# Node-row products of a graph kernel: the table in two float32r parts, and the cycles that use them

## The chip, the cores and the metric

The kernel runs on 1 core of one Trainium2 chip. The metric is the device time of one execution in microseconds (us), as the median of several runs.

## The reference, cut to what matters

There are 3125 nodes with 128 features and 53125 edges, sorted by their target node. The layer that is computed is

```python
row, col = (edge_index[0], edge_index[1])
h = jnp.concatenate([x[row], edge_attr], axis=1)
h = jax.nn.relu(_bn(h @ W1 + b1, g1, be1))
s = jax.ops.segment_sum(h, col, num_segments=n)
...
agg = jnp.where(cnt > 0, s / jnp.maximum(cnt, 1.0), 0.0)
h2 = jnp.concatenate([x, agg], axis=1)
h2 = jax.nn.relu(_bn(h2 @ W2 + b2, g2, be2))
return jax.nn.relu(h2 @ Wl + bl)
```

and the result is the layer norm of x plus that. `_bn` is a batch norm over all rows, so the mean and variance over all edges must be known before the segment sums start.

## The kernel before, in words

Since `x[row] @ W1x` is the same as picking rows of `x @ W1x`, the kernel first forms the table y = x W1x (3125 rows of 128), keeps it in SBUF as `ysb` and writes it to DRAM as `ytab`. The edges are then handled in 26 cycles (`NI`) of 4 groups (`U`), a group being 4 tiles of 128 edges: 416 tiles in all. For a tile, the rows of y come in one of three ways:

- the 12 tiles of the first three groups are gathered from x itself (line 642), before the table is ready;
- most others are gathered from `ytab` by an indirect DMA that GpSimd issues (`gather`, line 660), one instruction for each tile, all in one fixed order over cycles and groups;
- in the cycles of `NODES`, one or two tiles of group 2 (`NODEQ`) are not gathered. `node_onehots` (VectorE, line 1243) compares the node number of each edge with each of the 25 slices of nodes, which gives a one-hot matrix of 125 rows for each slice, in five batches; `node_rows` (TensorE, line 757) multiplies the 25 slices of `ysb` with them and sums in PSUM; `rows_out` (ScalarE, line 1039) copies the sum; `rows_back` (line 765) turns it and adds it to the edge product. Before, a pair of tiles is handled so in cycles 2 to 15 and a single one in cycles 16 to 19: 32 tiles.

In each group TensorE multiplies the edge attributes (`product`, line 744), VectorE adds the gathered rows (`make_h`, lines 1219, 1227, 1228 and 1230) and sums h and its squares (1251, 1258), and ScalarE makes the squares (984). `gather(i, q)` waits until the h of the same group of the cycle before is made (`h_ready`), so GpSimd can be up to four groups ahead of VectorE. In cycles 1 to 14 one more product for each cycle, x W2x for a part of the nodes (`x_product`, line 817), is made and copied by `x_product_out` (998). `onehots` (1209) makes the one-hots of the targets; from cycle 2 on it reads its constants from PSUM, where `keep_in_psum` (1289, 1290) puts them in cycle 1.

After the last cycle come the statistics, then the segment sums (line 890, from 497 us on), then the node part and the output. This second half is not touched.

The order of work on each engine is written out by hand, with semaphores between them. SBUF is full: the table, the one-hots and the node numbers lie in the tail of `res`, in slots that later cycles fill with h.

Of the kernel before, what the change touches and what calls it, by code (L numbers as in the profile page):

```python
# [26 lines left out]
F32 = mybir.dt.float32  # L27
BF16 = mybir.dt.bfloat16
I32 = mybir.dt.int32
ALU = mybir.AluOpType  # L30
ACT = mybir.ActivationFunctionType
AX_X = mybir.AxisListType.X

P = 128
# [5 lines left out]
KEEP = 3  # L40
# [3 lines left out]
EARLY = 3  # L44
QUAD = 32
ROWS0 = 2
ROWS1 = 20
PAIRS1 = 16
NODEQ = 2


# [5 lines left out]
def gnn_kernel(nc, E, x, xt, src, src_rows, dst, dst_rows, ea, W1, b1, g1, be1, W2, b2, g2, be2, Wl, bl, out):  # L57
    N, F = x.shape
    NI, FE = ea.shape[0], ea.shape[1] // 2
    H2 = W2.shape[1] // P  # L60
    NT = 25
    PN = N // NT
# [13 lines left out]
    BATCH = [(t, min(4, NT - t)) for t in range(0, NT, 4)]  # L76
# [10 lines left out]
    with ctx:  # L87
        def sb(name, shape, dt=F32):
            return ctx.enter_context(nc.sbuf_tensor(name, shape, dt))
# [4 lines left out]
        def sem(name):  # L94
            return ctx.enter_context(nc.semaphore(name))

        GF = TILES * F
        res = sb("res", [P, NI * KEEP * GF])
        work = sb("work", [P, 6, GF])
        away = [work[:, 0, :], work[:, 1, :]]  # L100
# [43 lines left out]

        at = NI * KEEP * GF

        def tail(n):
            nonlocal at
            at -= n
            return res[:, at:at + n]  # L150

        ysb = tail(NT * F)
        NODES = range(ROWS0, ROWS1)
        NODEAT = [P * sum(node_tiles(m) for m in range(i)) for i in range(ROWS1 + 1)]
        srcz = tail(NODEAT[-1] // 2).bitcast(BF16)
        TAB0 = at
        xt0 = tail(N)
        XT0 = at
# [43 lines left out]
        XW = XP * NT  # L202
        XSTEPS = [(h, k, min(XP, PN - k)) for k in range(0, PN, XP) for h in range(H2)]
# [1 line left out]
        h2x = agg[:, 3 * GF:3 * GF + XW]  # L205
        xgt = [agg[:, (1 + k) * GF:(2 + k) * GF] for k in range(2)]
        sq = [agg[:, (4 + k) * GF:(5 + k) * GF] for k in range(2)]
        assert XW <= 512 and len(XSTEPS) <= XT0 // (KEEP * GF) - 1

        psT = [pb(f"psT{i}", [P, 512]) for i in range(2)]  # L210
        psH = [pb(f"psH{i}", [P, GF]) for i in range(2)]
# [4 lines left out]
        psP = [psH[0], psH[1], psT[0], psC[1]]  # L216
# [3 lines left out]
        nodep = psC[0][0:PN, (U + 1) * WIN:(U + 1) * WIN + NT]  # L220
        NODECUT = [(t, t + 5) for t in range(0, NT, 5)]
        NB5 = len(NODECUT)
        NODEROWS = 12
        srcn = res[:, NODEROWS * KEEP * GF:NODEROWS * KEEP * GF + NODEAT[-1]]
        LONE = TAB0 - NT * P
        lone_hot = res[:, LONE:TAB0]
        pair_hot = res[:, LONE - 2 * NT * P:LONE]
        assert LONE - 2 * NT * P >= PAIRS1 * KEEP * GF and LONE >= ROWS1 * KEEP * GF
        assert NODEROWS * KEEP * GF + NODEAT[-1] <= PAIRS1 * KEEP * GF

        def node_chunk(i, b):

            t0, t1 = NODECUT[b]
            w = node_tiles(i) * P
            return (pair_hot if i < PAIRS1 else lone_hot)[0:PN, t0 * w:t1 * w]

# [39 lines left out]
        s_ysb = sem("y_ready")  # L276
        s_zr = sem("zeros_ready")
        s_tab = sem("table_written")
        x_ps = sem("w2_x_psum")
        x_out = sem("w2_x_copied")  # L280
        x_saved = sem("w2_x_saved")
# [14 lines left out]
        cnt_placed = sem("cnt_rows_placed")  # L296
# [413 lines left out]
        def _(pe):  # L710
# [10 lines left out]
            for b, (t0, n) in enumerate(BATCH):  # L721
# [7 lines left out]
                for t in range(n):  # L729
                    last = pe.matmul(psH[b % 2][0:PN, t * F:(t + 1) * F], xtv[:, t0 + t, :], w1x[:, :],  # L730
                                     start=True, stop=True)
# [5 lines left out]
            def product(i, par, nth, q):  # L737
                g = U * i + q
                if q == 0:
                    pe.wait_ge(ea_loaded[par], 16 * nth)  # L740
                pe.wait_ge(h_ready, g - U + 1)
                more = q == NODEQ and i in NODES
                for b in range(2):
                    last = pe.matmul(psP[q][:, b * 2 * F:(b + 1) * 2 * F], ea_cols(par, q, b),  # L744
                                     w1e[:, :, :].rearrange("p a f -> p (a f)"), start=(b == 0 or not more),
                                     stop=not more)
                last.then_inc(prod_ready, 1)

            def node_rows(i):

                w = node_tiles(i) * P
                pe.wait_ge(h_ready, U * (i - 1) + 2)
                for b, (t0, t1) in enumerate(NODECUT):
                    pe.wait_ge(nhot_ready, NB5 * (i - ROWS0) + b + 1)
                    for t in range(t0, t1):
                        k = (t - t0) * w
                        last = pe.matmul(psP[1][:, 0:w], ysb[0:PN, t * F:(t + 1) * F], node_chunk(i, b)[:, k:k + w],  # L757
                                         start=(t == 0), stop=(t == NT - 1))
                    last.then_inc(nhot_used, 1)

            def rows_back(i):
# [40 lines left out]
            def counts(i, par):  # L802

                pe.wait_ge(hotb_ready, i + 1)
                if i:
                    pe.wait_ge(cnt_placed, i)
                    pe.wait_ge(x_out, min(i, len(XSTEPS)))
                for j in range(TILES):
                    last = pe.matmul(psT[1][:, 0:U * WIN].rearrange("p (q w) -> p q w", q=U), onesb[:, :],  # L809
                                     hot[par][:, :, j * WIN:(j + 1) * WIN], start=(j == 0), stop=(j == TILES - 1))  # L810
                last.then_inc(cnt_ps, 1)

            def x_product(m):

                h, k, n = XSTEPS[m]
                pe.wait_ge(cnt_placed, m + 1)
                pe.matmul(psT[1][:, 0:n * NT].rearrange("o (p t) -> o p t", t=NT), w2x[:, h * P:(h + 1) * P],  # L817
                          xtv[:, :, k:k + n].rearrange("f t p -> f p t"), start=True, stop=True).then_inc(x_ps, 1)

            def edge_step(i, par, nth):  # L820
                if i in NODES:
                    node_rows(i)
                else:
                    product(i, par, nth, 1)
                if i <= len(XSTEPS):
                    x_product(i - 1)
                product(i, par, nth, 2)
                product(i, par, nth, 3)
                if i + 1 < NI:
                    product(i + 1, 1 - par, (i + 1) // 2 + 1, 0)  # L830
                counts(i, par)
                if i in NODES:
                    pe.wait_ge(rows_kept, i - ROWS0 + 1)
                    product(i, par, nth, 1)
                    rows_back(i)
# [32 lines left out]
            for j in range(TILES):  # L868
                h = away[1][:, j * F:(j + 1) * F]
                pe.matmul(gram, h, h, start=False, stop=False)  # L870
                last = pe.matmul(psT[0][:, 0:1], h, ones[:, :], start=False, stop=(j == TILES - 1))
# [29 lines left out]
            with pe.Else():  # L901
# [3 lines left out]
                          stop=True).then_inc(g_base, 1)  # L905
                with pe.Fori(0, NG) as g:
                    with pe.Fori(0, NB) as b:
                        pe.wait_ge(g_m, g + 1)
                        pe.wait_ge(g_hot, NB * g + b + 1)
                        for j in range(TILES):  # L910
                            pe.matmul(psH[0][:, 0:WIDE], mx[:, 0, j * F:(j + 1) * F], ghot[:, j * WIDE:(j + 1) * WIDE],
                                      start=(j == 0), stop=(j == TILES - 1))
                        for j in range(TILES):
                            last = pe.matmul(psH[1][:, 0:WIDE], onesf,
                                             ghot[:, j * WIDE:(j + 1) * WIDE], start=(j == 0), stop=(j == TILES - 1))
# [5 lines left out]
            for h in range(H2):  # L921
                last = pe.matmul(psX[:, 2 * F + h:2 * F + h + 1], w2[:, h * P:(h + 1) * P], c(C_U), start=True,
                                 stop=True)
# [39 lines left out]
        def _(act):  # L963
# [5 lines left out]
            for b, (t, n) in enumerate(BATCH):  # L969
                act.wait_ge(s_yps, b + 1)  # L970
                act.activation(ysb[0:PN, t * F:(t + n) * F], psH[b % 2][0:PN, 0:n * F], ACT.Copy).then_inc(s_ysb, 1)

            def x_rows_out(q):

# [5 lines left out]
            def squares(i, q):  # L980

                g = U * i + q
                act.wait_ge(h_ready, g + 1)
                act.activation(sq[g % 2], slot(i, i % 2, q), ACT.Square).then_inc(sq_ready, 1)  # L984

            def hot_out(i, par):

                act.wait_ge(hotb_ready, i + 1)
                act.dma_start(hot_dram[bass.ds(i, 1), :, :].rearrange("a p w -> (a p) w"),
                              hot[par][:, :, :].rearrange("p q w -> p (q w)")).then_inc(hot_saved[par], 16)  # L990

            def x_product_out(m):

                h, k, n = XSTEPS[m]
                act.wait_ge(x_ps, m + 1)
                if m:
                    act.wait_ge(x_saved, 16 * m)
                act.activation(h2x[:, 0:n * NT], psT[1][:, 0:n * NT], ACT.Copy).then_inc(x_out, 1)
                act.wait_ge(x_out, m + 1)
                act.dma_start(h2x_dram[:, h, k * NT:(k + n) * NT], h2x[:, 0:n * NT]).then_inc(x_saved, 16)  # L1000
# [40 lines left out]
            for i in range(1, NI - 1):  # L1041
                if i in NODES:
                    rows_out(i)
                if i <= len(XSTEPS):
                    x_product_out(i - 1)
                squares(i, 0)
                hot_out(i, i % 2)
                place_counts(i)
                for q in range(1, U):
                    squares(i, q)  # L1050
# [101 lines left out]
        def _(dve):  # L1152
# [132 lines left out]
            def keep_in_psum():  # L1285

                dve.wait_ge(xg_copied, EARLY)
                dve.wait_ge(s_node, 1)
                dve.tensor_copy(iotap, iota[:, :])
                dve.tensor_scalar(nodep, nodeid[0:PN, :], nodeid[0:PN, 0:1], -1.0, ALU.subtract, ALU.mult  # L1290
                                  ).then_inc(consts_kept, 1)
                dve.wait_ge(consts_kept, 1)
                dve.wait_ge(s_srcz, 1)

# [240 lines left out]
```

## Time and profile before

| | |
|---|---|
| Median of 3 runs | 634.95 us (634.64 to 634.95) |
| Profiled execution, first to last instruction (span) | 631.8 us |
| TensorE matmul busy | 503.7 us, 80% |
| VectorE busy | 464.6 us, 74% |
| GpSimd busy | 403.6 us, 64% |
| ScalarE busy | 201.2 us, 32% |
| Granted TensorE clock, mean | 0.873 of full speed |

The time of the profiled execution outside its span is not given; the median of the runs is 3.1 us above the span. Busy time leaves out what an engine spends on issuing and waiting. TensorE runs at the full clock from 55 to about 310 us, in a mix of both levels to about 376 us, at half clock to about 485 us, and at full again in the second half.

### The profile page before, as it was taken

What the parts mean: (1) busy time and instruction counts of PE and PEld (TensorE: products, weight loads), DVE (VectorE), ACT (ScalarE), POOL (GpSimd) and SP (SyncE); (2) the same over time, 40 slices, a digit from 0 to 9 for tenths busy, and PEclk for the clock granted to TensorE, in tenths of its full rate; (3) what the DMA queues carried; (4) which work ended last, traced back from release to release, by engine and by line L of the source; (5) the groups of instructions that cost most, each with busy time, mean ns of one, the idle gap of its engine ahead of it and who ended that gap; (6) DMA issues with size and microseconds to landing.
All of it is one profiled execution on the core that took longest, in us unless ns stands there. A gap on an engine that the chain in (4) does not pass through costs nothing.

```text
span 631.8 us, 9631 instructions
## 1 busy us (share of the span) xinstructions
PE 503.7 (80%) x2681; PEld 412.7 (65%) x2681; DVE 464.6 (74%) x720; ACT 201.2 (32%) x537; POOL 403.6 (64%) x507
## 2 busy tenths in 40 slices
PE   4749999999999999997866634444456899999984
PEld 4637778777777778886664422222223799999674
DVE  4789988888888998987666454454444777777786
ACT  2242222222222222222211211121114566666475
POOL 4777777777777777777777777777777133333500
PEclk9879999999999999999777755555557999999997
DMA  7953344434443434444334342334224277777103
GB/s 202 324 167 121 115 135 135 137 117 138 137 122 116 126 111 138 126 121 121 102 119 121 87 150 78 96 118 121 85 70 120 74 235 228 223 237 231 33 2 101
DMA packets 47608, 84.35 MB, mean 133 GB/s; under 512 B 11721, under 2 KB 23288, under 8 KB 47447
## 3 DMA queue, kind: packets, MB, share of 16 engines
q1 hardware_dynamic: 28834, 47.98, 23.6%
q0 software_dynamic: 12288, 25.19, 15.9%
q10 hardware_dynamic: 6453, 10.79, 4.8%
q8 instruction: 15, 0.25, 0.2%
q14 instruction: 18, 0.15, 0.1%
HBM read 63.82 MB, written 20.08 MB: 133 GB/s over the span
## 4 chain that ended last, share of the span: by engine, by line
PE 53%; POOL 24%; issue 9%; DVE 8%; DMA 3%; ACT 1%; SPq 1%; POOLq 0%; ACTq 0%; DVEq 0%
PE psH L757 25%; POOL res L660 17%; PE psH L890 7%; PE psC L890 7%; POOL work L660 7%; PE psH L744 4%; PE psT L817 3%; PE psT L744 2%; PE psC L744 2%; DVE res L1230 2%; DMA work<-ytab,srci 2%; DVE res L1387 1%; PE psT L809 1%; DMA w1x<-in_L_gnn_W 1%; DVE res L1243 1%
## 5 line engine op out<-in xcount | busy, mean ns | idle before, releaser
L660 POOL DMA_INDIRECT res<-ytab,srci x268 | 253.9, 947 | 81.7 <-issue 79.5
L757 PE MATMUL psH<-res 125*128 125x256 f32 (+1 forms) x900 | 178.7, 359 | 7.0 <-DVE res L1230 7.0
L757 PEld LDWEIGHTS psH<-res 125*128 125x128 f32 x900 | 154.9, 191 | 28.0 <-DVE res L1230 10.7
L660 POOL DMA_INDIRECT work<-ytab,srci x104 | 98.2, 944 | 31.7 <-issue 31.4
L1243 DVE TENSOR_TENSOR res<-res,psC 125x1280 f32<-125x1280 bf16 (+1 forms) x90 | 116.8, 1333 | 0.8 <-ACT res L1030 0.8
L744 PE MATMUL psH<-w1e,work 128*128 128x256 f32 x200 | 69.0, 480 | 42.8 <-DVE res L1230 42.8
L984 ACT ACTIVATE agg<-res 128x512 f32<-128x512 f32 x78 | 49.1, 630 | 143.7 <-DVE res L1230 80.5
L1230 DVE TENSOR_TENSOR res<-psH,res 128x512 f32<-128x512 f32 x50 | 34.5, 689 | 76.5 <-DMA res<-ytab,srci 48.6
L1355 DVE TENSOR_TENSOR work<-res,psX 128x512 f32<-128x512 f32 x103 | 70.2, 687 | 19.5 <-PE psC L890 12.2
L744 PEld LDWEIGHTS psH<-w1e,work 128*128 128x128 f32 x200 | 44.4, 239 | 56.5 <-issue 42.5
L685 POOL TENSOR_TENSOR agg<-agg,srci 128x64 f32 x104 | 32.0, 308 | 70.9 <-ACT srci L1095 70.0
L1258 DVE TENSOR_TENSOR psX<-agg,psX 128x512 f32<-128x512 f32 x103 | 71.0, 689 | 0.0
L1251 DVE TENSOR_TENSOR psS<-res,psS 128x512 f32<-128x512 f32 x78 | 54.3, 696 | 2.7
L890 PE MATMUL psH<-work 128*128 128x128 f32 (+1 forms) x416 | 50.8, 275 | 1.5 <-DVE work L1355 1.5
L890 PE MATMUL psC<-work 128*128 128x128 f32 (+1 forms) x416 | 50.7, 275 | 0.0
L890 PEld LDWEIGHTS psH<-work 128*128 128x128 f32 x416 | 48.5, 192 | 1.9 <-DVE work L1355 1.2
L744 PE MATMUL psC<-w1e,work 128*128 128x256 f32 x100 | 32.7, 458 | 21.0 <-DVE work L1230 21.0
L890 PEld LDWEIGHTS psC<-work 128*128 128x128 f32 x416 | 48.5, 192 | 0.0
L744 PEld LDWEIGHTS psT<-w1e,work 128*128 128x128 f32 x100 | 22.2, 232 | 40.1 <-DVE res L1230 25.0
L744 PE MATMUL psT<-w1e,work 128*128 128x256 f32 x100 | 33.1, 462 | 16.4 <-DVE res L1230 13.4
L744 PEld LDWEIGHTS psC<-w1e,work 128*128 128x128 f32 x100 | 21.5, 226 | 30.0 <-DVE work L1230 27.0
L984 ACT ACTIVATE agg<-work 128x512 f32<-128x512 f32 x25 | 15.7, 630 | 77.5 <-DVE work L1230 77.5
(200 smaller groups left out, 518.7 us busy)
## 6 DMA issues: line engine op xcount, KB each, us to landing
work<-in_edge_attr SPq DMA_DIRECT2D x26, 512.0 KB, 3.7
spill<-work SPq DMA_DIRECT2D x26, 256.0 KB, 2.3
res<-spill SPq DMA_DIRECT2D x25, 256.0 KB, 3.1
res<-ytab,srci POOLq DMA_INDIRECT x268, 2.5
hot_dram<-hotb ACTq DMA_DIRECT2D x13, 256.0 KB, 2.7
hot_dram<-work ACTq DMA_DIRECT2D x13, 256.0 KB, 2.4
hotb<-hot_dram SPq DMA_DIRECT2D x13, 256.0 KB, 2.7
work<-hot_dram SPq DMA_DIRECT2D x13, 256.0 KB, 3.0
```

The lines of the kernel that those rows point to most:

```text
L660: pool.indirect_dma_start(rows[:, j * F:(j + 1) * F], None, ytab, bass.IndirectOffsetOnAxis(ap=srci[:, j, g:g + 1], axis=0)).then_inc(gath ...
L685: pool.tensor_tensor(w, w, wsum[:, q, :], ALU.add).then_inc(agg_added, 1)
L744: last = pe.matmul(psP[q][:, b * 2 * F:(b + 1) * 2 * F], ea_cols(par, q, b), w1e[:, :, :].rearrange("p a f -> p (a f)"), start=(b == 0 or ...
L757: last = pe.matmul(psP[1][:, 0:w], ysb[0:PN, t * F:(t + 1) * F], node_chunk(i, b)[:, k:k + w], start=(t == 0), stop=(t == NT - 1))
L817: pe.matmul(psT[1][:, 0:n * NT].rearrange("o (p t) -> o p t", t=NT), w2x[:, h * P:(h + 1) * P], xtv[:, :, k:k + n].rearrange("f t p -> f p ...
L890: last = pe.matmul(psA[q][:, 0:n], mx[:, q, j * F:(j + 1) * F], hotf[:, q, j * WIN:j * WIN + n], start=(j == 0), stop=(j == TILES - 1))
L984: act.activation(sq[g % 2], slot(i, i % 2, q), ACT.Square).then_inc(sq_ready, 1)
L1230: dve.tensor_tensor(h, psP[q][:, :], h, ALU.add).then_inc(h_ready, 1)
L1243: dve.tensor_tensor(node_chunk(i, b).rearrange("p (t e) -> p t e", t=t1 - t0), srcz[0:PN, NODEAT[i]:NODEAT[i] + w].unsqueeze(1).broadcast_ ...
L1251: last = dve.tensor_tensor(psS[:, :], slot(i, par, q), psS[:, :], ALU.add)
L1258: last = dve.tensor_tensor(psX[:, :], sq[g % 2], psX[:, :], ALU.add)
L1355: dve.tensor_tensor(tiles(mx[:, q, :]), tiles(hin), negu, ALU.max).then_inc(m_ready, 1)
```

## The change

- The table is kept as two parts of type float32r in a new tile `table`: part 0 is a copy of `ysb` rounded to that type (ScalarE, right after `ysb` is complete), part 1 is the difference of `ysb` and part 0 (VectorE, in `keep_in_psum`). The one-hots are float32r too. `node_rows` issues two matmuls for each slice of nodes, one for each part, where it issued one in float32.
- The second part takes 3200 more columns of SBUF. With them the cycles move: pairs in cycles 2 to 13 (`PAIRS1` 14), singles in cycles 14 to 17 (`ROWS1` 18): 28 tiles.
- `x_product` runs twice in each of the cycles 1 to 7, where it ran once in each of the cycles 1 to 14. The second one comes after `product(i, 3)`; ScalarE copies it after the square of group 0.
- `ysb` and the node numbers (`srcn`) move to other places of `res`.

```diff
-ROWS1 = 20
-PAIRS1 = 16
+ROWS1 = 18
+PAIRS1 = 14
...
-        ysb = tail(NT * F)
+        tail(2 * NT * F)
+        table = nc.alloc_sbuf_tensor_at("node_table", [P, 2, NT * F], F32R, offset=res_at + 4 * at)
...
-        lone_hot = res[:, LONE:TAB0]
-        pair_hot = res[:, LONE - 2 * NT * P:LONE]
+        lone_hot = nc.alloc_sbuf_tensor_at("lone_hot", [P, NT * P], F32R, offset=res_at + 4 * LONE)
+        pair_hot = nc.alloc_sbuf_tensor_at("pair_hot", [P, 2 * NT * P], F32R, offset=res_at + 4 * (LONE - 2 * NT * P))
+        YAT = 20
+        ysb = res[:, YAT * GF:YAT * GF + NT * F]
...
-                        last = pe.matmul(psP[1][:, 0:w], ysb[0:PN, t * F:(t + 1) * F], node_chunk(i, b)[:, k:k + w],
-                                         start=(t == 0), stop=(t == NT - 1))
+                        for part in range(2):
+                            last = pe.matmul(psP[1][:, 0:w], table[0:PN, part, t * F:(t + 1) * F],
+                                             node_chunk(i, b)[:, k:k + w], start=(t == 0 and part == 0),
+                                             stop=(t == NT - 1 and part == 1))
...
-                    pe.wait_ge(x_out, min(i, len(XSTEPS)))
+                    pe.wait_ge(x_out, min(2 * i, len(XSTEPS)))
...
-                if i <= len(XSTEPS):
-                    x_product(i - 1)
+                if 2 * i <= len(XSTEPS):
+                    x_product(2 * i - 2)
                 product(i, par, nth, 2)
                 product(i, par, nth, 3)
+                if 2 * i <= len(XSTEPS):
+                    x_product(2 * i - 1)
...
+            act.wait_ge(s_ysb, len(BATCH))
+            act.activation(table[0:PN, 0, :], ysb[0:PN, :], ACT.Copy).then_inc(s_high, 1)
...
-                if i <= len(XSTEPS):
-                    x_product_out(i - 1)
+                if 2 * i <= len(XSTEPS):
+                    x_product_out(2 * i - 2)
                 squares(i, 0)
+                if 2 * i <= len(XSTEPS):
+                    x_product_out(2 * i - 1)
...
                 dve.tensor_scalar(nodep, nodeid[0:PN, :], nodeid[0:PN, 0:1], -1.0, ALU.subtract, ALU.mult
                                   ).then_inc(consts_kept, 1)
+                dve.wait_ge(s_high, 1)
+                dve.tensor_tensor(table[0:PN, 1, :], ysb[0:PN, :], table[0:PN, 0, :], ALU.subtract)
```

## Rows read from the trace of the kernel before

**Rows 1.** The page: chain that ended last, shares of the span.
```profile
PE 53%; POOL 24%; issue 9%; DVE 8%; DMA 3%; ACT 1%; SPq 1%; POOLq 0%; ACTq 0%; DVEq 0%
```

**Rows 2.** The chain in order of time, three of its pieces: start us, us, what.
```profile
170.29 11.06 PE psH L757 x50
187.91 11.06 PE psH L757 x50
...
256.96 11.06 PE psH L757 x50
273.18 11.06 PE psH L757 x50
```

**Rows 3.** Windows, gathers of line 660 alone: stretch, its length, busy (count), clock.
```profile
31.90:187.95 156.05, 117.97 (x125) 0.98 0.43 131
187.98:289.09 101.11, 76.44 (x81) 1.00 0.42 124
289.10:487.60 198.50, 150.05 (x159) 0.64 0.36 107
```

**Rows 4.** Groups by line, GpSimd: count, busy, mean ns, idle before and releasers.
```profile
L660 POOL DMA_INDIRECT res<-ytab,srci x268 | 253.9, 947 | 81.7 <-issue 79.5 <-DVE work L1230 0.9 <-DVE res L1230 0.9
L660 POOL DMA_INDIRECT work<-ytab,srci x104 | 98.2, 944 | 31.7 <-issue 31.4 <-DVE res L1230 0.3
```

**Rows 5.** Timeline, 20 to 47 us, GpSimd and VectorE: start us, us, engine, line.
```profile
20.55 0.94 POOL L642 DMA_INDIRECT res<-in_x,srci  x1 [0.30 <-DVE col L1196]
21.11 1.23 DVE L1209 TENSOR_TENSOR hotb<-iota,loc 128x1024 bf16<-128x1024 f32 x1
21.80 1.35 POOL L642 DMA_INDIRECT res<-in_x,srci  x1 [0.30 <-issue]
23.45 0.95 POOL L660 DMA_INDIRECT work<-ytab,srci  x1 [0.30 <-issue]
...
29.58 1.22 DVE L1209 TENSOR_TENSOR work<-iota,loc 128x1024 bf16<-128x1024 f32 x1
29.70 1.91 POOL L660 DMA_INDIRECT res<-ytab,srci  x1 [0.30 <-issue]
31.91 0.94 POOL L660 DMA_INDIRECT res<-ytab,srci  x1 [0.30 <-issue]
...
38.15 0.94 POOL L660 DMA_INDIRECT res<-ytab,srci  x1 [0.30 <-issue]
38.17 0.24 DVE L1290 TENSOR_SCALAR psC<-nodeid 125x25 f32<-125x25 f32 x1
39.25 7.08 DVE L1243 TENSOR_TENSOR res<-res,psC 125x1280 f32<-125x1280 bf16 x5 [0.84 <-ACT res L1030]
39.40 0.94 POOL L660 DMA_INDIRECT res<-ytab,srci  x1 [0.30 <-issue]
...
46.25 0.68 DVE L1230 TENSOR_TENSOR res<-psH,res 128x512 f32<-128x512 f32 x1
```

**Rows 6.** Timeline, the last gather and the add that waits for it.
```profile
487.62 0.94 POOL L660 DMA_INDIRECT work<-ytab,srci  x1 [0.30 <-issue]
...
490.32 0.69 DVE L1230 TENSOR_TENSOR work<-psC,work 128x512 f32<-128x512 f32 x1 [1.19 <-DMA work<-ytab,srci]
```

**Rows 7.** ScalarE: its timeline around 20 us, and a group by line.
```profile
16.83 0.81 ACT L971 ACTIVATE res<-psH 125x512 f32<-125x512 f32 x2 [0.28 <-PE psH L730]
21.44 0.60 ACT L978 ACTIVATE agg<-psC 128x512 f32<-128x512 f32 x1 [3.81 <-PE psC L781]
...
L1070 ACT ACTIVATE agg<-cnt,ones 128x1664 f32<-128x1664 f32 x2 | 3.3, 1674 | 0.0
```

**Rows 8.** Groups by line and form: count, busy, mean ns, idle before.
```profile
L1243 DVE TENSOR_TENSOR res<-res,psC 125x1280 f32<-125x1280 bf16 x70 | 101.2, 1481 | 0.8 <-ACT res L1030 0.8
L1243 DVE TENSOR_TENSOR res<-res,psC 125x640 f32<-125x640 bf16 x20 | 15.6, 815 | 0.0
```

**Rows 9.** Windows, all engines: PE, PEld, DVE, ACT, POOL busy (count), clock, DMA.
```profile
170.30:187.90 17.60, 17.27 (x76) 13.79 (x76) 15.81 (x20) 4.34 (x11) 13.21 (x14) 1.00 0.41 127
364.00:384.00 20.00, 9.12 (x20) 5.29 (x20) 10.33 (x16) 3.38 (x8) 15.10 (x17) 0.53 0.38 122
```

**Rows 10.** Timeline of one pair cycle and its neighbour.
```profile
169.55 0.69 DVE L1230 TENSOR_TENSOR res<-psH,res 128x512 f32<-128x512 f32 x1 [1.66 <-PE psH L744]
...
176.76 0.94 POOL L660 DMA_INDIRECT res<-ytab,srci  x1 [0.30 <-DVE work L1230]
...
203.28 0.60 PE L809 MATMUL psT<-hotb,onesb 128*128 128x256 bf16 x4
```

**Rows 11.** Timeline, the first gather of group 1 in cycle 2.
```profile
54.38 0.94 POOL L660 DMA_INDIRECT res<-ytab,srci  x1 [0.30 <-issue]
```

More of the change, by code:

```diff
@@ L29 @@
 I32 = mybir.dt.int32
+F32R = mybir.dt.float32r
 ALU = mybir.AluOpType
@@ L97, in gnn_kernel @@
         GF = TILES * F
+        res_at = -(-nc.sbuf_base // 32) * 32
         res = sb("res", [P, NI * KEEP * GF])
@@ L207, in gnn_kernel @@
         sq = [agg[:, (4 + k) * GF:(5 + k) * GF] for k in range(2)]
-        assert XW <= 512 and len(XSTEPS) <= XT0 // (KEEP * GF) - 1
+        assert XW <= 512 and len(XSTEPS) % 2 == 0 and len(XSTEPS) // 2 <= XT0 // (KEEP * GF) - 1
         psT = [pb(f"psT{i}", [P, 512]) for i in range(2)]
@@ L222, in gnn_kernel @@
         NB5 = len(NODECUT)
-        NODEROWS = 12
+        NODEROWS = 11
         srcn = res[:, NODEROWS * KEEP * GF:NODEROWS * KEEP * GF + NODEAT[-1]]
         LONE = TAB0 - NT * P
-        lone_hot = res[:, LONE:TAB0]
-        pair_hot = res[:, LONE - 2 * NT * P:LONE]
+        lone_hot = nc.alloc_sbuf_tensor_at("lone_hot", [P, NT * P], F32R, offset=res_at + 4 * LONE)
+        pair_hot = nc.alloc_sbuf_tensor_at("pair_hot", [P, 2 * NT * P], F32R, offset=res_at + 4 * (LONE - 2 * NT * P))
+        YAT = 20
+        ysb = res[:, YAT * GF:YAT * GF + NT * F]
+        assert YAT * GF + NT * F <= NODEROWS * KEEP * GF
         assert LONE - 2 * NT * P >= PAIRS1 * KEEP * GF and LONE >= ROWS1 * KEEP * GF
@@ L278, in gnn_kernel @@
         s_tab = sem("table_written")
+        s_high = sem("table_high_ready")
         x_ps = sem("w2_x_psum")
@@ L815, in x_product @@
                 h, k, n = XSTEPS[m]
-                pe.wait_ge(cnt_placed, m + 1)
+                pe.wait_ge(cnt_placed, m // 2 + 1)
+                if m % 2:
+                    pe.wait_ge(x_out, m)
                 pe.matmul(psT[1][:, 0:n * NT].rearrange("o (p t) -> o p t", t=NT), w2x[:, h * P:(h + 1) * P],
```

## The prediction, made before the changed kernel was run

> **What bounds the kernel now.** I began with the chain that ended last. It gives TensorE over half the span [rows 1], and in time order it is one node product of 11.06 us after another, 17.6 us apart and later 16.2 us apart [rows 2]. Read alone, this says that cheaper node products shorten the kernel. So I looked next at whoever else is never free. GpSimd is "busy" only 64%, but the windows that count its gathers alone say more [rows 3]: 125 gathers in 156.05 us, 81 in 101.11 us, 159 in 198.50 us, which is 1.248 us for each in all three stretches, while TensorE's clock goes from full to 0.64. The groups by line show why it looks idle: 372 gathers of 0.946 us, and before nearly every one 0.30 us put down to "issue"; the few releases put down to VectorE make 2.1 us in 372 and are the same 0.30 each [rows 4]. From 23.45 us to the last gather at 487.62 us [rows 5, 6] the queue never waits for another engine. Its pace is 464.17 us for 371 steps; less the one long step (29.70 to 31.91, 2.21 us [rows 5]) it is 461.96/370 = 1.2485 us.
>
> The chain shows TensorE because a pair cycle has 14 gathers, 14 x 1.2485 = 17.48 us, and TensorE takes 17.61 [rows 2]: it lags by 0.13 us more each cycle, and the chain prefers the later one. But that lag never reaches the queue. The gather at 176.76 may start once the h of the same group of the cycle before is made, and that was made by 169.55 + 0.69 = 170.24 [rows 10]: 6.5 us of cover. After the x products end, TensorE needs 16.2 us and catches up. So up to 488 us the time is a count: gathers times 1.2485 us, plus whatever makes one gather longer.
>
> **The change, part by part.**
>
> *Four more gathers.* 28 tiles come from node products where 32 did; the other 4 are gathered: 376 instead of 372. 4 x 1.2485 = **+5.0 us** on the queue, with nothing to cover it: behind the last gather comes the add at 490.32 that waits for its landing [rows 6], and the statistics.
>
> *The split on VectorE.* The new subtraction (125 x 3200, both inputs in SBUF) has two effects. Its length: the one-hot instruction takes 1.481 us at 1280 columns and 0.815 at 640 [rows 8], 1.04 ns a column, so 1.48 + 1920 x 0.00104 = 3.48 us. It runs right behind L1290 (38.17 to 38.41 [rows 5]), from about 38.3 or 38.4 to 41.8 or 41.9. So the one-hots start 2.6 us later than 39.25, and h of group 1 of cycle 1 is ready at about 46.25 + 0.68 + 2.6 = 49.5 [rows 5]; the gather that waits for it starts at 54.38 [rows 11]. Hidden, with 4.8 us to spare, and VectorE then has 15.8 us of work in 17.6 [rows 9] and catches up.
>
> The other effect is on the gathers themselves. Three kinds of length stand in rows 5: 0.94, 1.35 and 1.91. The two long ones are those that start while L1209 reads `iota` and `loc`, both in SBUF: VectorE ends at 21.11 + 1.23 = 22.34 and 29.58 + 1.22 = 30.80, the gathers end at 23.15 and 31.61, both 0.81 us behind it. The gather at 20.55 was under way when L1209 began and kept 0.94. So a gather wants something that this instruction holds, about 0.94 - 0.81 = 0.13 us after its start, and waits for its end. The later L1209s read the constants from PSUM, and no gather in rows 3 is longer. For the subtraction: the gather at 38.15 wants it at 38.28, the next one starts at 39.40. If the first is through, the next ends at 41.8 + 0.81 = 42.6 where it ended at 40.34: **+2.3 us**. If the subtraction is first, the one at 38.15 is caught: it ends at 42.6 instead of 39.09, +3.5 us. The two starts are some 0.1 us apart; I take the first, since L1290 is still running at 38.28, and keep both.
>
> The Trainium skill (SBUF — State Buffer, section Who interferes with whom) says that a VectorE instruction with two SBUF inputs blocks a GpSimd instruction that reads SBUF, but also that a tensor_tensor was not seen to stall the descriptor generation of a DMA. The rows speak for the first (by it 7.3 us in all); by the second the sum would be 5.0.
>
> *The copy on ScalarE.* 3200 elements; 1664 take 1.67 us [rows 7], so about 3.1 us. ScalarE is free from 17.64 to 21.44, 3.8 us of idle [rows 7]: hidden with 0.7 us left. If it were longer by a microsecond, the first h would come later, still ahead of its gather.
>
> *float32r products.* Not in the trace. A float32 product of 256 columns counts as two entries of 0.221 us (11.06/50 [rows 2]); now each part is one product, again 50 a cycle. Lower bound: the bfloat16 product of 256 columns, four in 0.60 us [rows 10], 0.15 each, 50 x 0.15 = 7.5 us. Upper bound: each still costs what float32 costs, 0.442 us, 22.1 us. I take the lower, 3.6 us less for TensorE than now, as the nearest row for one pass. It brings nothing, as the queue is ahead. It decides only when TensorE's cycle passes 17.48 us: it is 17.61 now, and 1.4 more with a second x product (17.61 - 16.21 [rows 2]), so in cycles 2 to 7 at 17.48 = 19.0 - 11.06 + 50 t, t = 0.191 us. If nothing changed at all (t = 0.221), cycles 2 to 7 would lag 1.5 us each, 9 us in all, against the 6.5 us of cover: some 2.7 us more.
>
> *One-hots in float32r.* Same columns, still 4 bytes: 0. VectorE has 17.48 - 15.81 = 1.67 us spare in a pair cycle [rows 9], so the five instructions could each be 0.33 us longer (1.81 for 1.48) before this shows.
>
> *x products in seven cycles.* Their second wait on ScalarE's copy sits ahead of product(i+1, 0), counts and product(i, 1) on TensorE; behind those waits only the h of group 1, which has the 6.5 us cover. ScalarE is 4.3 us busy in 17.6 [rows 9]. 0. The tail behind the last gather stays.
>
> *The clock.* With fewer columns TensorE may be granted the half clock at times, as later (0.53, 9.1 us busy in 20 [rows 9]). The queue kept 1.248 us there. At half clock all of a pair cycle would take about 2 x (19.0 - 11.06 + 7.5) = 31 us, more than 17.48, so TensorE would then be busy without a pause, and in the rows such stretches have the full clock: a passing lag, within the cover.
>
> **Sum.** 5.0 + 2.3 = 7.3 us. Span 631.8 + 7.3 = 639.1; the median stands 3.1 us above the span, so 634.95 + 7.3 = **642.2 us**, slower by 1.1%.
>
> **Rivals.** A measurement of this kernel can tell about 0.2%, 1.3 us, from no change.
>
> 1. *Forecast*: the queue counts, and the subtraction holds one gather. 642.2, or 643.4 if it catches the one at 38.15. Chance 0.72.
> 2. *The subtraction holds nothing*: only the four gathers, 634.95 + 5.0 = 639.9. For it: only two gathers in rows 5 show the hold. Against: both end the same 0.81 us behind VectorE. Chance 0.12.
> 3. *TensorE or VectorE takes over*: float32r products over 0.191 us, or slower one-hots. At t = 0.221, 642.2 + 2.7 = 645; at 0.442, a pair cycle takes 17.61 - 11.06 + 22.1 = 28.65, 12 x 11.2 = 134 us more, and 6 x 1.4 = 8 for the x products: about 784. Chance 0.09, mostly near the low end.
> 4. *Faster*: the shorter node products relieve the gathers. For it: the chain names TensorE in the pair cycles. Against: a gather costs 1.248 beside a full TensorE and a half empty one [rows 3]. It decides from 1.2485 x 372/376 = 1.235 us a gather if the hold is nil; with it, 8.6 us (7.3 and 1.3) must come from 376 gathers, 0.023 us each, a step of 1.226 us; then 633.6. Chance 0.04.
> 5. *No change*: something covers the four gathers, such as ScalarE's last copies ending later than the last add. The add at 490.32 is waited for directly [rows 6]. Chance 0.03.
>
> Slower 0.93, same 0.03, faster 0.04. The range takes in rivals 1 and 2 and the low end of 3: 639.4 to 645.0.
>
> **What would show it right or wrong.** In the profile after: 376 gathers at 1.2485 us; one of about 3.2 us near 39.4 (or 4.4 at 38.15); node products far shorter than 11.06 us; the last gather near 494.9; the chain in the pair cycles naming GpSimd. If the gather near 39.4 takes 0.94, rival 2 holds; if releases by VectorE of more than 0.3 us appear in GpSimd's idle time, rival 3. The forecast is wrong if the pace of the gathers depends on something that the change touches and that these windows do not vary.

## The result, and the profile after

The changed kernel takes 642.07 us (641.81 to 642.31, 4 runs), against 634.80 us for the kernel before in the same comparison: a ratio of 1.0126, 95% interval 1.0109 to 1.0143. It is slower by 7.3 us; 642.2 us was predicted.

The page of the changed kernel, its first line, the shares of the chain that ended last, and some groups (count, busy and mean; idle before and releasers):

```profile
span 640.5 us, 9412 instructions
...
POOL 51%; PE 20%; issue 17%; DVE 6%; DMA 4%; ACT 1%; POOLq 0%; ACTq 0%; DVEq 0%
...
L765 PE MATMUL psH<-pair_hot,node_table 125*128 125x256 f32 x600 | 82.1, 301 | 18.0 <-DVE res L1247 18.0
...
L1260 DVE TENSOR_TENSOR pair_hot<-res,psC 125x1280 fp32r<-125x1280 bf16 x60 | 86.6, 1479 | 0.0
```

The chain has gone from TensorE 53% [rows 1] to GpSimd 51%, while TensorE's busy time fell from 503.7 to 452.4 us. TensorE has nearly gone from the first half of the chain, and yet the kernel ends later. The one-hots cost what they cost (1479 ns for 1481 [rows 8]). The groups of GpSimd's gathers:

```profile
L667 POOL DMA_INDIRECT res<-ytab,srci x272 | 260.7, 959 | 82.9 <-issue 82.3 <-DVE res L1245 0.6
L667 POOL DMA_INDIRECT work<-ytab,srci x104 | 98.2, 944 | 31.7 <-issue 30.8 <-DVE res L1247 0.9
```

376 gathers for 372 [rows 4], the waits the same 0.30 us each, and a mean of 959 ns for 947 in one group: some gather is much longer. The timeline near 38 us shows it:

```profile
38.04 0.23 DVE L1307 TENSOR_SCALAR psC<-nodeid 125x25 f32<-125x25 f32 x1
38.19 3.48 DVE L1310 TENSOR_TENSOR node_table<-res,node_table 125x3200 fp32r<-125x3200 f32 x1
38.29 4.20 POOL L667 DMA_INDIRECT res<-ytab,srci  x1 [0.30 <-issue]
...
42.79 0.94 POOL L667 DMA_INDIRECT res<-ytab,srci  x1 [0.30 <-issue]
```

The subtraction takes 3.48 us. The gather that starts 0.10 us behind it takes 4.20 us instead of 0.94 and ends at 42.49, 0.82 us behind the subtraction, as both long gathers of rows 5 ended 0.81 us behind theirs. The end of the first half, to be read against rows 6:

```profile
496.13 0.94 POOL L667 DMA_INDIRECT work<-ytab,srci  x1 [0.30 <-issue]
...
499.03 0.69 DVE L1247 TENSOR_TENSOR work<-psC,work 128x512 f32<-128x512 f32 x1 [1.44 <-DMA work<-ytab,srci]
```

The last gather starts 8.51 us later than before (487.62 [rows 6]; 494.9 was forecast for it): 4 x 1.2485 = 4.99 for the count, 4.20 - 0.94 = 3.26 for the held gather, and 0.26 for small shifts in the first 32 us and in the steps. The span is 8.7 us longer, the median only 7.3. In every execution of this study for which both are known, 1.7 to 2.1 us lie outside the span, so the profiled execution of before, with its 631.8 us, took some 633.6 us and was about 1.3 us faster than its median.

### The profile page after: what moved, and what is told of

The parts are those of the page before. It is cut to its first block, busy times and chain, and to the rows that moved or that the text cites. A ratio compares the mean times of both kernels' runs of the same rounds, so it can differ in the third digit from the quotient of the medians.

```text
span 640.5 us, 9412 instructions
## 1 busy us (share of the span) xinstructions
PE 452.4 (71%) x2573; PEld 366.1 (57%) x2573; DVE 455.5 (71%) x709; ACT 202.6 (32%) x536; POOL 411.1 (64%) x511
## 4 chain that ended last, share of the span: by engine, by line
POOL 51%; PE 20%; issue 17%; DVE 6%; DMA 4%; ACT 1%; POOLq 0%; ACTq 0%; DVEq 0%
POOL res L667 36%; POOL work L667 13%; PE psH L903 7%; PE psC L903 7%; DMA res<-ytab,srci 2%; POOL res L649 2%; PE psH L751 1%; PE psH L765 1%; DVE res L1406 1%; DMA srci<-in_src 1%; DMA work<-ytab,srci 1%; DVE res L1247 1%; PE psT L828 1%; PE psT L968 1%; PE psH L968 1%
## 5 line engine op out<-in xcount | busy, mean ns | idle before, releaser
L667 POOL DMA_INDIRECT res<-ytab,srci x272 | 260.7, 959 | 82.9 <-issue 82.3
L751 PE MATMUL psH<-w1e,work 128*128 128x256 f32 x200 | 77.2, 526 | 74.3 <-DVE res L1247 74.3
L751 PEld LDWEIGHTS psH<-w1e,work 128*128 128x128 f32 x200 | 47.7, 262 | 103.7 <-issue 86.1
L765 PE MATMUL psH<-pair_hot,node_table 125*128 125x256 f32 x600 | 82.1, 301 | 18.0 <-DVE res L1247 18.0
L765 PEld LDWEIGHTS psH<-pair_hot,node_table 125*128 125x128 f32 x600 | 79.6, 209 | 20.5 <-DVE res L1247 20.5
L1260 DVE TENSOR_TENSOR pair_hot<-res,psC 125x1280 fp32r<-125x1280 bf16 x60 | 86.6, 1479 | 0.0
L751 PE MATMUL psC<-w1e,work 128*128 128x256 f32 x100 | 37.3, 510 | 28.6 <-DVE work L1247 28.6
L751 PE MATMUL psT<-w1e,work 128*128 128x256 f32 x100 | 35.3, 487 | 24.8 <-DVE res L1247 21.5
L751 PEld LDWEIGHTS psC<-w1e,work 128*128 128x128 f32 x100 | 23.2, 249 | 40.6 <-DVE work L1247 37.3
L1027 ACT ACTIVATE cnt<-psT 1x64 f32 x104 | 22.4, 216 | 62.9 <-PE psT L818 39.9
```

What stands on the lines that cost most here:

```text
L667: pool.indirect_dma_start(rows[:, j * F:(j + 1) * F], None, ytab, bass.IndirectOffsetOnAxis(ap=srci[:, j, g:g + 1], axis=0)).then_inc(gath ...
L765: last = pe.matmul(psP[1][:, 0:w], table[0:PN, part, t * F:(t + 1) * F], node_chunk(i, b)[:, k:k + w], start=(t == 0 and part == 0), stop= ...
L1027: last = act.activation(cnt[r:r + 1, bass.ds(bases[q], WIN)], psT[1][r:r + 1, q * WIN:(q + 1) * WIN], ACT.Copy)
L1260: dve.tensor_tensor(node_chunk(i, b).rearrange("p (t e) -> p t e", t=t1 - t0), srcz[0:PN, NODEAT[i]:NODEAT[i] + w].unsqueeze(1).broadcast_ ...
```

## The experiments

The seven kernels were timed in two batches, each on one chip together with the kernel before. Its median was 634.29 us in the batch of four (float32 with 28 tiles, two x products, pieces, subtraction twice) and 634.37 in the batch of three. Each cost over before is the difference of medians within a batch. The changed kernel was not timed again with them: where one of them is compared with its 642.07 us, the medians of the kernel before differ by 0.4 to 0.5 us, and the figure against each one's own kernel before is given too.

**The moved cycles without float32r.** The kernel before with 28 tiles and two x products a cycle, on TensorE and in ScalarE's copies. (The x products must be doubled for it: the one-hots of the first single cycle lie where `xt0` lay and wait for the last x product, which would come too late.)

```diff
-ROWS1 = 20
-PAIRS1 = 16
+ROWS1 = 18
+PAIRS1 = 14
...
-                if i <= len(XSTEPS):
-                    x_product(i - 1)
+                if 2 * i <= len(XSTEPS):
+                    x_product(2 * i - 2)
                 product(i, par, nth, 2)
                 product(i, par, nth, 3)
+                if 2 * i <= len(XSTEPS):
+                    x_product(2 * i - 1)
...
```

> The kernel before with the cycles of the change (28 tiles, two x products a cycle) but with the float32 table and float32 one-hots: no split, node products of 11.06 us. If the count of gathers sets the time, 4 x 1.2485 = 5.0 us over before, about 639.8 us, and 376 gathers in the profile with none over 2 us. If the node products on TensorE set the time, this kernel must be slower than the changed one (642.1), by up to 12 x 4.8 = 58 us, since its node products take 11.06 us where the changed kernel's take 6.26. The rival in which TensorE's lag eats the cover (19.0 us a cycle in cycles 2 to 7) gives up to 2.7 us more, 642.5.

Measured: 642.96 us (641.80 to 647.83), ratio 1.0146 (1.0118 to 1.0174), 8.7 us over before; just above 642.5, the upper end of what was expected. So TensorE's 4.8 us a cycle are not worth 58 us, and 5.0 of the 8.7 are the gathers, if each costs its step. Beside them the trace has two real waits, 3.9 us beyond the usual 0.30 each. This is the longer one, in GpSimd's timeline:

```profile
142.63 0.94 POOL L660 DMA_INDIRECT res<-ytab,srci  x1 [0.30 <-issue]
145.92 0.95 POOL L660 DMA_INDIRECT res<-ytab,srci  x1 [2.35 <-DVE res L1236]
```

A gather that waits 2.35 us, 2.05 more than the others, for an h that TensorE's lag made late. The changed kernel has no such row. In this trace the steps of the gathers also took 1.251 us instead of 1.2485, 0.9 us in all, for a reason that no run shows.

**Two x products a cycle, alone.** The same x-product edits on the kernel before, with its 32 tiles.

> The kernel before with two x products in each of cycles 1 to 7 and nothing else changed (32 tiles, float32). TensorE's pair cycle grows from 17.6 to about 19.0 us in cycles 2 to 7, with a lag of 1.5 us a cycle, 9 us in all against 6.5 us of cover. If the cover is as read, 0 to 2.7 us over before, 634.8 to 637.5. If the second wait on ScalarE's copy reaches the gathers each cycle, more than that. Gathers: 372 at 1.2485 us.

Measured: 639.28 us, ratio 1.0082 (1.0070 to 1.0094), 5.0 us over before; outside what was expected. Its chain between 107 and 147 us (start us, us, what), and one of the three gathers that wait:

```profile
107.93 11.06 PE psH L757 x50
118.99 1.88 PE psT L819 x2
...
122.59 1.88 PE psT L819 x2
...
127.49 11.06 PE psH L757 x50
```

```profile
127.70 0.94 POOL L660 DMA_INDIRECT res<-ytab,srci  x1 [2.39 <-DVE res L1236]
```

A pair cycle takes 127.49 - 107.93 = 19.56 us, not 19.0: the second x product costs 1.95 us (19.56 - 17.61), about its 1.88. In the rows left out stand only products on TensorE, one add on VectorE (0.70 us) and 0.06 us of issue: the second wait for ScalarE's copy, the other cause named in the expectation, is not in the chain. I had read 1.4 from 17.61 - 16.21 [rows 2], but the cycles that are 16.2 us apart still hold a small x product, of 125 columns where the others have 500. TensorE's timeline of the kernel before, between the node products of rows 2:

```profile
251.65 0.64 PE L817 MATMUL psT<-res,agg 128*128 128x125 f32 x2
...
267.86 0.64 PE L817 MATMUL psT<-res,agg 128*128 128x125 f32 x2
```

With 19.56 the lag is 19.56 - 17.48 = 2.08 us a cycle. The waits put down to VectorE in this kernel sum to 6.6 us over three gathers, 5.7 beyond the usual 0.30 each. What the cover was is read at the first gather of group 1 in cycle 3 and the h of the cycle before that it needs. First the kernel before, then this one, then the one with 28 tiles:

```profile
63.86 0.69 DVE L1230 TENSOR_TENSOR res<-psH,res 128x512 f32<-128x512 f32 x1 [1.73 <-PE psH L744]
71.85 0.94 POOL L660 DMA_INDIRECT res<-ytab,srci  x1 [0.30 <-issue]
```

```profile
68.07 0.69 DVE L1236 TENSOR_TENSOR res<-psH,res 128x512 f32<-128x512 f32 x1 [3.19 <-PE psH L744]
71.68 0.94 POOL L660 DMA_INDIRECT res<-ytab,srci  x1 [0.30 <-issue]
```

```profile
66.74 0.69 DVE L1236 TENSOR_TENSOR res<-psH,res 128x512 f32<-128x512 f32 x1 [3.19 <-PE psH L744]
71.99 0.94 POOL L660 DMA_INDIRECT res<-ytab,srci  x1 [0.30 <-issue]
```

The cover is 7.30 us before, 2.92 here and 4.56 with 28 tiles: the second x products of cycles 1 and 2 have taken most of the difference before the waits begin. From that h to the one of cycle 6 there are four cycles of lag, 8.3 us (both x products of cycle 7 are small). A gather that waits starts some 0.3 us after its h, so 2.92 - 0.27 = 2.65 us of cover can be used up, and 8.3 - 2.65 = 5.7 is what was measured. The 1.6 us more of cover with 28 tiles go with waits that are 1.8 us shorter; what makes it more there was not looked into.

**The subtraction in seven pieces.**

```diff
-                dve.tensor_tensor(table[0:PN, 1, :], ysb[0:PN, :], table[0:PN, 0, :], ALU.subtract)
+                for a in range(0, NT * F, 512):
+                    z = min(a + 512, NT * F)
+                    dve.tensor_tensor(table[0:PN, 1, a:z], ysb[0:PN, a:z], table[0:PN, 0, a:z], ALU.subtract)
```

> The changed kernel with the subtraction cut into seven instructions of at most 512 columns, the same work in all. If a VectorE instruction with two inputs in SBUF holds a gather until the instruction ends, a piece of 0.69 us can hold one gather by at most 0.7 us each, and the gather of 4.20 us near 38.3 shrinks to 0.94 to 1.7: about 1.5 to 3 us under the changed kernel, 639.3 to 640.6. If the gather is held by the whole backlog of VectorE, pieces or not, nothing changes: 642.1. If the long gather has another cause, 642.1 as well.

Measured: 640.01 us, ratio 1.0087 (1.0074 to 1.0100), 5.7 us over before and 2.1 us under the changed kernel (1.6 under, each against its own kernel before). VectorE and the gathers beside it:

```profile
39.46 3.98 DVE L1312 TENSOR_TENSOR node_table<-res,node_table 125x512 fp32r<-125x512 f32 x7
39.96 0.99 POOL L667 DMA_INDIRECT res<-ytab,srci  x1 [0.30 <-issue]
41.26 0.95 POOL L667 DMA_INDIRECT res<-ytab,srci  x1 [0.30 <-issue]
```

VectorE works longer (3.98 us for 3.48) with no pause between the pieces, and the gathers keep 0.95 to 0.99 us. The one at 39.96 ends at 40.95, 0.81 us behind the first piece, which ends at 40.14 while the others still have to run: a waiting gather gets in between two instructions. The one at 41.26 starts together with a piece and is not held at all; that piece takes 0.72 us instead of 0.68. Against the float32 kernel with the same 28 tiles and x products, timed in the same batch, it is 2.95 us faster: that is what the lighter float32r products are worth here, with the hold nearly gone.

**The subtraction twice.** The second writes its result, which nobody reads, beside `ysb`.

```diff
                 dve.tensor_tensor(table[0:PN, 1, :], ysb[0:PN, :], table[0:PN, 0, :], ALU.subtract)
+                dve.tensor_tensor(res[0:PN, 20 * GF + NT * F:20 * GF + 2 * NT * F], ysb[0:PN, :], table[0:PN, 0, :], ALU.subtract)
```

> The changed kernel with a second subtraction of the same size behind the first, its result not used. If the hold lasts for one instruction and the gather gets in between, the next gather is held by the second one: about 2.2 us more, 644.3. If the waiting gather does not get in between, it is held for both: 3.4 more, 645.5. If the hold is no cost of the subtraction, no change, since VectorE's extra 3.4 us lies within the cover: 642.1.

Measured: 644.03 us (642.71 to 645.62), ratio 1.0155 (1.0139 to 1.0170), 2.0 us over the changed kernel (2.5 over, each against its own kernel before).

```profile
38.25 3.48 DVE L1310 TENSOR_TENSOR node_table<-res,node_table 125x3200 fp32r<-125x3200 f32 x1
38.41 4.13 POOL L667 DMA_INDIRECT res<-ytab,srci  x1 [0.30 <-issue]
41.65 3.49 DVE L1311 TENSOR_TENSOR res<-res,node_table 125x3200 f32<-125x3200 f32 x1
42.85 3.11 POOL L667 DMA_INDIRECT res<-ytab,srci  x1 [0.30 <-issue]
```

Two gathers are held, each by one instruction: the first gets through at the seam at 41.7 and the second, started at 42.85, is held by 3.11 - 0.94 = 2.17 us until 0.82 us behind the second subtraction (45.14).

**A long instruction added to the kernel before, with two SBUF inputs, and with one.** Its result is not used.

```diff
                 dve.wait_ge(consts_kept, 1)
+                dve.tensor_tensor(res[0:PN, 20 * GF:20 * GF + NT * F].rearrange("p (t f) -> p t f", f=WIN),
+                                  ysb[0:PN, :].rearrange("p (t f) -> p t f", f=WIN),
+                                  iota[0:PN, :].unsqueeze(1).broadcast_to([PN, 2 * NT, WIN]), ALU.subtract)
                 dve.wait_ge(s_srcz, 1)
```

The other kernel has `iotap`, the same constants in PSUM, in the place of `iota`.

> The kernel before with one added VectorE subtraction of 125 x 3200 elements in keep_in_psum, with both inputs in SBUF (the constants iota as second input), its result not used. If such an instruction holds a gather until it ends, one gather near 38 to 40 us takes 3.2 to 4.3 us and the kernel is 2.3 to 3.4 us over before, 637.1 to 638.2. If only VectorE's lost time counted, it is hidden in the cover: 634.8.

> As the run with two SBUF inputs, but the second input is the copy of the same constants in PSUM. Same columns, so about the same 3.5 us on VectorE. If two SBUF inputs make the hold, every gather near it keeps 0.94 us and the time is that of before, 634.8. If the length of the instruction makes it, the time is that of the other run.

Measured: 636.88 us, ratio 1.0043 (1.0029 to 1.0057), with two SBUF inputs; 633.32 us, ratio 0.9992 (0.9983 to 1.0001), with one. First the timeline of the former, then that of the latter:

```profile
38.64 3.49 DVE L1293 TENSOR_TENSOR res<-res,iota 125x3200 f32<-125x3200 f32 x1
38.75 4.20 POOL L660 DMA_INDIRECT res<-ytab,srci  x1 [0.30 <-issue]
```

```profile
39.07 3.49 DVE L1293 TENSOR_TENSOR res<-res,psC 125x3200 f32<-125x3200 f32 x1
39.13 0.94 POOL L660 DMA_INDIRECT res<-ytab,srci  x1 [0.30 <-issue]
40.38 0.94 POOL L660 DMA_INDIRECT res<-ytab,srci  x1 [0.30 <-issue]
```

The same 3.49 us on VectorE: 4.20 us for a gather in the one, 0.94 in the other. It is where the second input lies that decides whether a gather is held; being busy for as long does not. The two kernels lie 3.6 us apart. And 3.5 us of VectorE at this place are free, though they use up cover: in cycle 13 the gather of group 1 starts 2.47 us after the h that it needs (246.40, 243.93), where it was 5.97 before (246.67, 240.70).

**A version that beats both.** The changed kernel with two bfloat16 parts of 2 bytes a value in the place of two of 4, with bfloat16 one-hots (`pair_hot` and `lone_hot`) and the seven pieces, and with the SBUF that this frees given to more cycles. How many bits of the table either pair of parts keeps was not measured.

```diff
-ROWS1 = 18
-PAIRS1 = 14
+ROWS1 = 21
+PAIRS1 = 18
...
-        tail(2 * NT * F)
-        table = nc.alloc_sbuf_tensor_at("node_table", [P, 2, NT * F], F32R, offset=res_at + 4 * at)
+        tail(NT * F)
+        table = nc.alloc_sbuf_tensor_at("node_table", [P, 2, NT * F], BF16, offset=res_at + 4 * at)
...
         TAB0 = at
+        tail(NT * P // 2 + NT * P)
...
```

> The changed kernel with the table as two bfloat16 parts (16 bits of it are kept instead of 24) and bfloat16 one-hots, the subtraction in seven pieces, and the SBUF that this frees used for more cycles: pairs in cycles 2 to 17, singles in 18 to 20, 35 tiles. If the count of gathers sets the time, 369 gathers are 3.7 us under before and 8.7 under the changed kernel's share of gathers: 634.8 - 3.7 = 631.1, with up to 0.7 us for a piece that holds a gather, 631.8. If VectorE (15.8 us of work in a pair cycle of 17.48) or TensorE sets the pair cycles, more of them bring nothing: 634 or more.

Measured: 630.56 us, ratio 0.9943 (0.9930 to 0.9957): 3.8 us under before and 11.5 under the median of the changed kernel (11.1, each against its own kernel before). Two of its groups, GpSimd and VectorE:

```profile
L668 POOL DMA_INDIRECT res<-ytab,srci x265 | 251.0, 947 | 80.7 <-issue 79.5 <-DVE res L1248 0.6 <-DVE work L1248 0.3
...
L1261 DVE TENSOR_TENSOR pair_hot<-res,psC 125x1280 bf16<-125x1280 bf16 x80 | 115.6, 1480 | 0.0
```

265 + 104 = 369 gathers, none of which waits, and one-hots in bfloat16 cost VectorE 1480 ns, the same as in float32. Three gathers fewer than before are 3 x 1.2485 = 3.7 us of the 3.8: the gain is SBUF turned into fewer gathers.

All nine traces together: the first gather of line 642 (or its like) starts at 7.7 to 7.9 us in each, and the last gather starts where the count and the long steps put it: 487.62, plus 1.2485 for each gather beyond 372, plus the last two columns, is met within 0.6 us by all but the float32 kernel with 28 tiles (1.0, with its steps of 1.251 us). "Waits" are for h, "long" is what the longest held gather near 38 to 43 us takes over 0.94.

| kernel | gathers from the table | last starts | waits over 0.30 | long |
|---|---|---|---|---|
| before | 372 | 487.62 | none | none |
| changed | 376 | 496.13 | none | 3.26 |
| float32, 28 tiles | 376 | 497.46 | 3.9 | none |
| two x products | 372 | 493.05 | 5.7 | none |
| pieces | 376 | 493.17 | none | 0.05 |
| subtraction twice | 376 | 498.24 | none | 3.19 and 2.17 |
| long, two SBUF | 372 | 490.29 | none | 3.26 |
| long, one PSUM | 372 | 487.31 | none | none |
| bfloat16, 35 tiles | 369 | 484.17 | none | 0.50 |

## Why the prediction was right

**What bounds the kernel.** Right. From the first gather of the table on, the queue waits for no h in any kernel but the two that kept the heavy products beside two x products a cycle, and the time follows its count. The chain of before, which named TensorE, was about a lag inside the cover. The 6.5 us of cover were read in one cycle, though, and taken for all: in the trace of before they are 7.3 in cycle 3 and 6.0 in cycle 13.

**Four gathers, +5.0 us.** Right. The changed kernel with the subtraction in pieces has the four gathers and nearly no hold, and is 5.7 us over before. No run has the four gathers and nothing else, so 5.0 rests on the step of 1.2485 us and on the kernel with 369 gathers, 3.8 us under before for 3.7.

**The hold.** The mechanism is shown by the runs with two SBUF inputs and with one. The case was the wrong one of the two: I took the gather at 38.15 to be through (+2.3) and kept 3.5 as the other end. Both starts moved, the subtraction began at 38.19, before L1307 had ended, and the gather at 38.29; it was caught, +3.26 in the profiled execution. By medians the hold costs 642.07 - 640.01 = 2.1 us (1.6, each against its own kernel before), and the same hold on the kernel before costs 2.5 us, or 3.6 against the kernel with one SBUF input; the median of the changed kernel alone does not tell 2.3 from 3.3. Between the traces of the changed kernel and of the one with pieces, the 3.2 us of hold shrink to 2.4 us of span: the run with pieces is 0.4 us later at its gather near 38 us, after an early gather that waits 1.06 us, 0.8 more than the others, for the last write of the table, and it takes 0.6 us longer from the start of its last gather to the end (144.95 for 144.38). Why it does was not looked into. The sum of 7.3 met the measured 7.3, while the terms by the profile are 5.0, 3.3 and 0.4 against a profiled execution that was itself a fast one; so the agreement to 0.1 us is luck, the one to 1.5 us is not.

The Trainium skill (SBUF — State Buffer, section Who interferes with whom) has both answers: that a VectorE instruction with two SBUF inputs contends with a GpSimd instruction that reads SBUF, and that a probe did not see a tensor_tensor stall a DMA, with a reason marked there as inferred. For an indirect gather, whose indices lie in SBUF (`srci`), this trace agrees with the first (4.20 us against 0.94) and not with the second.

**The copy on ScalarE.** Right: 2.87 us, from 17.67 to 20.54, and no gather waits for what follows.

**float32r products.** Fifty in 6.26 us at a granted clock of 1.00, 0.125 us each. The lower bound that I took, 7.5 us, was too high: the four bfloat16 products of rows 10 start 0.11 us apart, and only the last one's 0.27 us makes them 0.60, so the row gives 0.11 us for one, not 0.15. Fifty bfloat16 node products take 5.63 us in the last kernel, 0.113 each. The measured 0.125 us is well under the 0.191 from which TensorE would decide (0.180 with the cycle of 19.56 us). "It brings nothing" was right against the kernel before, but incomplete: within this change it undoes the lag that doubling the x products causes. 2.95 us separate the float32 and the float32r kernel with the same tiles.

**x products in seven cycles.** The step that failed, had TensorE stayed as it was: I priced the second one at 1.4 us a cycle and the loss at 2.7 us, from rows in which an x product of 125 columns was left. It is 1.95 us, and alone it costs 5.0 us. Two more readings behind the 2.7 us were wrong, and in part made up for each other: five cycles lag, not six, and the cover is no fixed 6.5 us, since the second x products of cycles 1 and 2 bring it to 2.9 us by cycle 3. In the changed kernel they cost nothing because with the lighter products a cycle of TensorE takes 17.2 us on average (five cycles from 49.31 to 135.55 us), less than the 17.48 of the queue, and the cover is 8.1 us in cycle 3 and never less after it. The same lag cost 5.0 us with 32 tiles and about 3.7 with 28 (which varied from 641.8 to 647.8 us): in the traces the waits are 5.7 and 3.9, as the covers of 2.9 and 4.6 us in cycle 3 let expect.

**One-hots, clock, tail.** As forecast, 0. TensorE's mean clock fell from 0.873 to 0.814. It now falls in the pair cycles too: the node product at 67.22 us, before which TensorE had been idle for 3.48 us, takes 7.73 us at a granted clock of 0.78, where the next one, at 83.44, takes 6.27 at 1.00. No gather waits for it.

## What to carry to other kernels

Count the instructions of the engine that is never released by anyone, even when its busy share is low: here 1.2485 us a gather, with the holds and waits added, gave the start of the last gather in nine kernels within 1.0 us, while the chain of before pointed at TensorE. Before a table is made larger to make products cheaper, ask what the space was paying for; before an engine off the path is loaded, measure its cover in microseconds, where it is least, and the price of the added work in full size. Beside a queue of indirect gathers like this one, give a long VectorE tensor_tensor at most one SBUF input, or cut it into short pieces.

## What was not expected of the hardware

- Seven VectorE instructions back to back (3.98 us) hold a gather by 0.05 us, in the bfloat16 kernel by 0.50; one of the same columns (3.48 us) by 3.26: the waiting side gets its turn at a seam.
- A held gather ends 0.81 or 0.82 us after the instruction that held it, in all seven cases shown.
- The three gathers that start 0.10 to 0.16 us behind a long instruction with two SBUF inputs are held to its end; the one that starts together with a piece (both at 41.26) is not, and the piece takes 0.04 us longer.
- A float32 node product of 256 columns takes 0.442 us (11.06/25), a float32r one 0.125 (6.26/50).
